# A decoder's second attention on one core: where it begins behind the expert feed, and what runs in its first stages

## The reference, cut to what matters

```
x = layernorm(x + L0_attn(x))        # retention
x = layernorm(x + L0_xattn(x, ctx))  # attention to the context, then W_out
x = layernorm(x + L0_ffn(x))         # 64 experts, top 8 of each token, and 2 shared experts
x = layernorm(x + L1_attn(x))        # linear attention with a memory (64 wide)
x = layernorm(x + L1_xattn(x, ctx))  # keys = ctx @ W_k, values = ctx @ W_v, 16 heads
x = layernorm(x + L1_ffn(x))         # 8 gated experts, top 2 of each token
```

## Time and profile before

| | us |
|---|---|
| median of 3 runs | 1998.11 |
| lowest, highest | 1990.38, 2002.12 |
| profiled execution, its own time | 2008.36 |
| profiled execution, span of the core | 2005.4 |
| TensorE matmuls busy in the span | 1712.4 (85%) |
| VectorE busy | 1165.6 (58%) |
| ScalarE busy | 622.8 (31%) |
| GpSimd busy | 894.2 (45%) |
| mean granted clock of TensorE | 0.912 of full speed |

### The profile page before, as it was taken

One profiled execution on the slowest core, in us unless ns is written; L12 is line 12 of the kernel. 1 busy time (PEld: TensorE's weight loads), 2 busy tenths in 40 slices (PEclk: granted clock), 3 DMA queues, 4 the chain that ended last, 5 costly groups with the idle time before them and its releaser, 6 DMA issues.

```text
span 2005.4 us, 45537 instructions
## 1 busy us (share of the span) xinstructions
PE 1712.4 (85%) x17739; PEld 1345.2 (67%) x17739; DVE 1165.6 (58%) x3228; ACT 622.8 (31%) x957; POOL 894.2 (45%) x1000
## 2 busy tenths in 40 slices
PE   6788888888789889998998478999977499999994
PEld 5576666666556666675776356676656499999994
DVE  3576655665441276766656466787764345655564
ACT  1232322222231276454455123454332111111110
POOL 0017556754758102888887865333322202222223
PEclk9998988998699999999999688899987699999997
DMA  9415543555349799897999822114101512333332
GB/s 322 148 47 195 185 149 110 193 183 187 131 149 252 204 298 304 257 285 259 299 306 304 288 86 62 55 64 148 44 33 54 172 49 75 90 93 94 100 93 68
DMA packets 269634, 322.61 MB, mean 161 GB/s; under 512 B 25083, under 2 KB 245487, under 8 KB 268655
## 3 DMA queue, kind: packets, MB, share of 16 engines
q1 hardware_dynamic: 234559, 226.38, 35.7%
q0 software_dynamic: 33024, 92.32, 14.2%
q10 hardware_dynamic: 1840, 1.00, 0.2%
HBM read 157.22 MB, written 162.40 MB: 159 GB/s over the span
## 4 chain that ended last, share of the span: by engine, by line
PE 69%; DVE 8%; issue 6%; DMA 5%; POOL 4%; ACT 4%; another core or an unknown queue 2%; SPq 1%; DVEq 0%; POOLq 0%; ACTq 0%
PE wide L2065 13%; PE d_yp L2077 6%; PE wide L1197 4%; PE wide L110 4%; PE wide L127 4%; PE wide L1200 4%; PE bank L1210 3%; PE bank L1217 3%; PE e_yp L1737 3%; PE wide L1726 3%; PE bank L1031 2%; PE wide L1184 2%; POOL big L1439 2%; PE e_xp L1714 2%; PE bank L1174 2%
## 5 line engine op out<-in xcount | busy, mean ns | idle before, releaser
L1439 POOL DMA_INDIRECT big<-results,slots x256 | 263.2, 1028 | 208.6 <-DMA results<-e_y 128.5
L2065 PE MATMUL wide<-d_xt,d_ws 128*128 128x128 f32 x2272 | 278.0, 276 | 0.6 <-issue 0.6
L2065 PEld LDWEIGHTS wide<-d_xt,d_ws 128*128 128x128 f32 x2272 | 271.7, 193 | 4.5 <-issue 1.0
L597 POOL DMA_INDIRECT lists<-big,slots x160 | 159.3, 995 | 117.7 <-DVE slots L959 71.3
L661 ACT ACTIVATE pt<-wide 77x2048 f32<-77x2048 f32 x64 | 119.9, 1873 | 216.0 <-PE wide L1200 125.0
L1934 POOL DMA_INDIRECT d_picked<-results,slots x64 | 64.1, 1002 | 181.1 <-DMA results<-d_y 167.8
L1965 ACT ACTIVATE d_gate<-wide 128x512 f32<-128x512 f32 x71 | 42.4, 597 | 324.2 <-PE wide L2065 319.6
L1454 DVE SCALAR_TENSOR_TENSOR big<-big,weights 128x256 f32<-128x256 f32 x256 | 109.2, 488 | 43.8 <-DMA big<-results,slots 30.0
L2077 PE MATMUL d_yp<-d_wd,d_h 128*128 x568 | 134.2, 379 | 0.0
L110 PE MATMUL wide<-shared_sx,shared_sw 128*128 128x512 f32 x256 | 127.4, 621 | 5.4 <-DMA shared_sx<-res_t 2.9
L127 PEld LDWEIGHTS wide<-shared_sw,shared_sh 128*128 128x128 f32 x512 | 98.1, 192 | 45.1 <-issue 29.3
(11 more groups left out here) (280 smaller groups left out, 3511.5 us busy)
## 6 DMA issues: line engine op xcount, KB each, us to landing
lists<-zero SPq DMA_DIRECT2D x20, 2048.0 KB, 14.8
e_x<-lists SPq DMA_DIRECT2D x80, 512.0 KB
results<-e_y SPq DMA_DIRECT2D x80, 512.0 KB
d_x<-lists SPq DMA_DIRECT2D x71, 128.0 KB
results<-d_y SPq DMA_DIRECT2D x71, 128.0 KB
e_w<-in_L_w SPq DMA_DIRECT2D x2, 4096.0 KB
shared_sw<-in_x_t SPq DMA_DIRECT2D x32, 128.0 KB
x<-in_x SPq DMA_DIRECT2D x8, 512.0 KB
```

The costliest lines, as they stand in the source:

```text
L597: pool.indirect_dma_start(out=lists, out_offset=bass.IndirectOffsetOnAxis(ap=slots[:, b, i, k:k + 1], axis=0), in_=z2[i % 3][:, b, :], in_ ...
L1439: pool.indirect_dma_start(out=picked[:, c % NG, b, :], out_offset=None, in_=results[0:-(-PAGES_OF_STEP[s] // 4) * 4 * R0, :], in_offset=ba ...
L2065: ins = mm(out[T % 2][:, a * P:(a + 1) * P], ws[:, T % NW, n, c, a * P:(a + 1) * P], xt[:, T % 2, c], start=c == 0, stop=c == KC - 1)
```

## The change

- The feed hands on `y_done` (last eviction done) in place of the landing of the last stores and of the shared experts' base; the stores' landing is waited for by VectorE at the first top. The sync queue's own waits for them at the feed's end go.
- The second attention's constants come in two lots. `consts_soon`: on the sync queue, behind x of step 0, ident, the three linear weights and the memory; on ScalarE's queue causal, gate, head_mask, mem_norm and the output weight. `consts`: context, wk, wv on the sync queue, the rest on ScalarE's. TensorE, ScalarE and VectorE begin behind the first lot; GpSimd waits for all at its first ln1, TensorE at the first key.
- The keys' products become jobs of the order, behind num (0, 1), x0t (1, 1), lv 1 and ct 0; TensorE waits for all four laid out before the first mx.
- One late sum (46) stands ahead of `begin_here` instead of three. 47 is behind tri (0, 1), 48 behind x0t (1, 1), 49 behind wo (0, 1), then three in a round for steps 0 to 4: behind x1t (i, 1), mx (i, 0) and mx (i, 3).

```diff
+def with_keys(order):
+    behind = [("num", 0, 1), ("x0t", 1, 1), ("lv", 1, 0), ("ct", 0, 0)]
+    out = []
+    for job in order:
+        out.append(job)
+        if job in behind:
+            out.append(("key", behind.index(job), 0))
+    return out
 def with_late(order):
-    behind = [("x0t", 0, 1), ("sig", 0, 0)]
-    for i in range(4):
-        behind += [("x1t", i, 1), ("q", i, 1), ("mx", i, 1), ("mx", i, 3)]
-    behind = behind[:STEPS * K0 + 1 - LATE - 3]
-    out, n = [], STEPS * K0 + 1 - len(behind)
+    behind = [("tri", 0, 1), ("x0t", 1, 1), ("wo", 0, 1)]
+    for i in range(5):
+        behind += [("x1t", i, 1), ("mx", i, 0), ("mx", i, 3)]
+    out, n = [], LATE + 1
...
-            loads = [context, (wk[:], col(d["wk"])), (wv[:], col(d["wv"]))] + loads
-            loads += [(wlin[:, :, 0], col(d["wq1"])), (wlin[:, :, 1], col(d["wk1"])), (wlin[:, :, 2], col(d["wv1"])),
-                      (mem_norm[:], d["mem_norm_rows"])]
-            others = [(gate[:], d["gate"])] + others + [(wq[:], col(d["wq"])), (iota[:], d["iota"])]
+            soon = [loads[0]] + [(wlin[:, :, n], col(d[w])) for n, w in enumerate(("wq1", "wk1", "wv1"))]
             for h in range(2):
                 rows_h = slice(h * MEM, (h + 1) * MEM)
-                others += [(wo[rows_h], d["wo1"])]
-                loads += [(memory[rows_h, 0:MEM], d["memory"]), (memory[rows_h, MEM:], d["mem_norm"])]
+                soon += [(memory[rows_h, 0:MEM], d["memory"]), (memory[rows_h, MEM:], d["mem_norm"])]
+            soon_too = [(causal[:], d["causal"]), (gate[:], d["gate"]), loads[1], (mem_norm[:], d["mem_norm_rows"])]
+            soon_too += [(wo[h * MEM:(h + 1) * MEM], d["wo1"]) for h in range(2)]
+            loads = [context, (wk[:], col(d["wk"])), (wv[:], col(d["wv"]))]
+            others = [(wq[:], col(d["wq"]))] + others[1:] + [(iota[:], d["iota"])]
...
             load_t(0)
+            if not first:
+                load(0)
             for dst_ap, src_ap in soon:
                 sp.dma_start(dst_ap, src_ap).then_inc(consts_soon, 16)
...
             if not first:
-                for n in range(LATE, LATE + 3):
-                    late_on_pool(pool, n)
+                late_on_pool(pool, LATE)
             begin_here(pool)
...
                 if stage == "ln1" and not first:
+                    if i == 0:
+                        pool.wait_ge(consts, CONSTS)
...
+            for dst_ap, src_ap in soon_too:
+                act.dma_start(dst_ap, src_ap).then_inc(consts_soon, 16)
...
-                act.wait_ge(consts, CONSTS)
+                act.wait_ge(consts_soon, SOON)
...
             if not first:
-                for n in range(LATE, LATE + 3):
-                    late_on_vector(dve, n)
+                late_on_vector(dve, LATE)
             begin_here(dve)
...
+                if stage == "key":
+                    ps = filled(dve, job)
+                    lay_out_keys(i, ps[:, 0:KC * CTX].rearrange("p (c k) -> p c k", c=KC), ps[0:CTX, DM:2 * DM])
...
                 if stage == "top":
+                    if i == 0:
+                        for of_before, count in stores:
+                            dve.wait_ge(of_before, count)
...
             begin_here(pe)
-            if first:
-                pe.wait_ge(consts_soon, 16 * len(soon))
-            else:
-                pe.wait_ge(consts, CONSTS)
-                for b in range(NB):
-                    out = take_bank(("key", b, 0))
...
+            pe.wait_ge(consts_soon, SOON)
...
-            else:
-                pe.wait_ge(ready, READY)
             for job in order:
...
+                if not first and job == ("key", 0, 0):
+                    pe.wait_ge(consts, CONSTS)
+                if not first and job == ("num", 0, 0):
+                    pe.wait_ge(ready, BEGUN)
+                if job == ("mx", 0, 0):
                     pe.wait_ge(ready, READY)
+                    for b in range(0 if first else NB):
+                        emptied(pe, ("key", b, 0))
...
             store_quad(QUADS - 1)
-            for n in range(NY):
-                sp.wait_ge(sent[n], 16 * len(range(n, QUADS, NY)))
-            sp.wait_ge(base_sent, 16 * STEPS)
...
-        return over, kept, late_on_pool, late_on_vector
+        return [(y_done, QUADS)], over, kept, late_on_pool, late_on_vector
```

More of the change, by code:

```diff
@@ L200, in with_late @@
             n += 1
+    assert n == STEPS * K0 + 1
     return out
@@ L229, in attention_phase @@
                     spare=None, route=None, block=None,
-                    over=(), kept=(), late_on_pool=None, late_on_vector=None, units=None):
+                    over=(), stores=(), kept=(), late_on_pool=None, late_on_vector=None, units=None):
     first = layer == 0
-    order = with_units(steady(SEQUENCE0)) if first else with_late(steady(SEQUENCE1))
-    prep_jobs = [] if first else [(("key", b, 0), "narrow") for b in range(NB)]
-    plan = Banks(prep_jobs + bank_jobs(order), {"wide": ["w"], "narrow": [0, 1, 2, 3]}, shared.uses)
+    order = with_units(steady(SEQUENCE0)) if first else with_late(with_keys(steady(SEQUENCE1)))
+    plan = Banks(bank_jobs(order), {"wide": ["w"], "narrow": [0, 1, 2, 3]}, shared.uses)
     score_scale = 1.0 if first else float(XD) ** -0.5
@@ L368, in attention_phase @@
         consts = sem("consts")
-        consts_soon = sem("consts_soon") if first else None
+        consts_soon = sem("consts_soon")
         ready = sem("ready")
@@ L472, in _ @@
             load_t(0)
+            if not first:
+                load(0)
             for dst_ap, src_ap in soon:
                 sp.dma_start(dst_ap, src_ap).then_inc(consts_soon, 16)
-            load(0)
+            if first:
+                load(0)
             for dst_ap, src_ap in loads:
@@ L723, in _ @@
             if first:
[L724 removed]
+                dve.wait_ge(consts_soon, SOON)
                 make(nc.vector.reciprocal(scale_qk[:, 2:4], scale_qk[:, 0:2]))
@@ L731, in lay_out @@
             def lay_out():
-                dve.wait_ge(consts, CONSTS)
+                if first:
+                    dve.wait_ge(consts, CONSTS)
+                else:
+                    dve.wait_ge(consts_soon, SOON)
                 make(nc.vector.tensor_reduce(mask2[:], head_mask[:].rearrange("p (m h) -> p h m", h=2), AX.X, ALU.add))
@@ L990, in _ @@
             begin_here(pe)
-            if first:
-                pe.wait_ge(consts_soon, 16 * len(soon))
-            else:
-                pe.wait_ge(consts, CONSTS)
-                for b in range(NB):
-                    out = take_bank(("key", b, 0))
-                    for g in range(KC):
-                        for c in range(KC):
-                            mm(out[:, g * CTX:(g + 1) * CTX], wk[:, c, g * P:(g + 1) * P], ctx_t[:, b, c],
-                               start=c == 0, stop=c == KC - 1)
-                    for c in range(KC):
-                        ins = mm(out[0:CTX, DM:2 * DM], ctx_t[:, b, c], wv[:, c], start=c == 0, stop=c == KC - 1)
-                    fills(ins, ("key", b, 0))
+            pe.wait_ge(consts_soon, SOON)
             if first:
                 pe.wait_ge(state_done, 1)
-            else:
-                pe.wait_ge(ready, READY)
             for job in order:
@@ L1027, in _ @@
                     out = take_bank(job)
+                if stage == "key":
+                    for g in range(KC):
+                        for c in range(KC):
+                            mm(out[:, g * CTX:(g + 1) * CTX], wk[:, c, g * P:(g + 1) * P], ctx_t[:, i, c],
+                               start=c == 0, stop=c == KC - 1)
+                    for c in range(KC):
+                        ins = mm(out[0:CTX, DM:2 * DM], ctx_t[:, i, c], wv[:, c], start=c == 0, stop=c == KC - 1)
+                    fills(ins, job)
                 if stage == "qk":
```

39 lines of the change are left out of this document (20 added, 19 removed).

## The result

| | before | after |
|---|---|---|
| median, 20 runs each, us | 2002.05 | 2009.37 |
| lowest, highest | 1990.38, 2010.85 | 2001.99, 2020.48 |
| profiled execution, its own time | 2008.36 | 2007.76 |
| span of the core | 2005.4 | 2005.7 |

The ratio is 1.0039, 95% interval [1.0025, 1.0054]: the kernel after is **slower by 0.4%**, some 7 us, where 9 us less was forecast, and outside the range.

The account below looks back on a forecast made before the run. No engine fills the span, so the prediction read the hand-over hole alone, where TensorE waits for loads. 11 us gained at the start less 2 lost in the rounds gave 9 us, a median of 1989 us, range 1980 to 1998.

Parts of the forecast that it names:

- Start of TensorE, 1127.5 (1126.5 to 1130): At the hand-over: TensorE begins at 1127.5 instead of 1137.43, taking 5.0 us from the last piece's issue to use.
- First stages at half clock, +2.7: Transposes and linear products before the numerator run on an unwarmed array, 2.7 us longer (bounds 0 and 4).
- Keys, 6.7 us: Four keys' products between numerator and output product lengthen TensorE's path by 6.7 us (bounds 5 and 12).
- ln1 of step 0 at 1161.1: First layernorm of step 0 taken up by GpSimd at 1161.1 instead of 1172.06, 11 us gained.
- Late sums three a round, 2 lost (bounds 6 lost, 1 gained): Dense rounds of steps 0 to 4: two more sums and a norm, spread thinner, lose 2 us.
- rival C: Start paid late: late first lot, keys at half clock, or GpSimd holding ln1; gain about 2 us, 1996; chance 0.23.
- Nothing at the end: Behind the rounds: the gated phase moves as a block; no loss at the kernel's end was priced.
- D: Slower: step 7's late store holds up the second weights and x of step 7; 10 us slower, 2008; chance 0.05.
- E: Second lot lands after 1145, so TensorE idles at key 0 instead; gain 3 to 5 us, 1994; chance 0.05.
- five rounds of 47 us or more: Sign that would prove the forecast wrong; rounds of steps 0 to 4 were expected at some 45 us each.

Follow-up runs that it names:

- e1: Kernel after with its late sums from the 50th on placed as in the kernel before, four a round; ratio 0.9971 to before.
- e2: Kernel before with only the late sums' places of the kernel after, three a round over five rounds; ratio 1.0095 to before.
- e8: Kernel after with eight more small memsets on idle GpSimd; ratio 1.0002 to before.
- e14: Kernel after with four late sums a round in steps 1 to 3, two of them where VectorE idles; ratio 0.9956 to before.
- e10: As e14, but the last late job (norm and store of step 7) moved into step 4's round; ratio 1.0021 to before.
- e16: The same kernel as e14, run on a chip where before takes 2015.9 us; ratio 1.0000 to before.
- e17: The same kernel as e10, run on a chip where before takes 2015.9 us; ratio 1.0035 to before.

## Why the prediction was wrong, point by point

*Start of TensorE, 1127.5 (1126.5 to 1130): inside the bounds.* 1128.60. The whole of this profile lies 0.8 us earlier than before's at this point (ScalarE's last eviction at 1114.41, not 1115.22), so the forecast on its time base is 1126.7. The last piece was issued at 1121.90, as forecast on that base (1121.7), but issue to use took 6.7 us instead of 5.0. By the Trainium skill's rule of interleaving (DMA: Bandwidth & Descriptors, "Issuing engines are not separate DMA queues") it would have been 1130; the trace lies between the two.

*First stages at half clock, +2.7: right.* The granted clock was 0.50 from 1128 to 1134 and 1.00 from 1136. The transposes took 1.94 for 1.09 and the linear products 4.87 for 2.81; from the start to the end of the numerator it was 12.9 us (1128.60 to 1141.53), 13.0 forecast. The Trainium skill's sentence that the default state is throttled (TensorE: Matmul & The Clock Gate, "What's actually happening") spoke against this change here, and the trace agrees.

*Keys, 6.7 us: too high by 2.6.* Numerator to output product took 13.3 us where before took 9.15, so 4.2. The keys' own 7.3 us of TensorE were priced right. What the sum left out is that the slow stretch of before is not there: the 16 linear products behind the second key took 1.95 us, 3.68 before, as the granted clock was 1.00 all along, where before it was 0.50 from 1160 to 1164. That the keys' work keeps it up is likely but not tried.

*ln1 of step 0 at 1161.1: right, in part by luck.* 1159.56, and GpSimd's last gather ahead of it ended at 1156.06, where I put it. Measured from the feed's last product 11.7 us were gained; forecast 11. The number is so close because two misses cancel: TensorE began 1.9 us late on the profile's own base, and the keys' stretch was 2.6 us shorter than forecast.

***Late sums three a round, 2 lost (bounds 6 lost, 1 gained): this is the step that failed.*** Five rounds cost 13.9 us more. By the medians the places of the late sums as a whole cost 10 us (after against e1, from different groups of runs, ratios 0.0068 apart) or 16 (e2 against before, 0.0095), each less 0.0016 for the tail. I wrote that "nearly the same work is spread thinner" and priced it by the us, from what I called two rounds of 47.3 us; the two maxima are the ends of one. It broke in three places:
- Each us of late work was priced by what it cost where four sums stood in a round, 0.74 us of path (5.9 for 8). In after, step 3's round has 6.4 us of it (three sums of 1.67 and the norm's 1.37) and is 7.5 longer than before's: 1.2 us of path for each. Step 4's has 3.0 us of it and is 5.0 longer. In step 3 one sum and the norm stand ahead of the second peak, in step 4 one sum, and TensorE's third maximum waits 3.0 and 3.2 us for it, 0.43 in before.
- The clock was left out of the rounds, though rival C had it at the start. Step 2's round holds three sums too and took 42.9 at 1.00; step 3's took 49.0 at 0.90. A mean of 0.90 is 9.8 us at 1.2 GHz, in which half the work is done: up to 4.9 us, my estimate, of the 6.1 between them; the norm's 1.4 could be the rest. The hole of 1.51 us stands right ahead of the fall; behind the one of 2.99 the clock stayed at 1.00 for another 9 us. So that the holes cost the clock is argued, not shown.
- I let the thinner rounds pay for the two new ones. Rounds 3 and 4, free in before, came in at 49.0 and 48.1 instead of 41.5 and 43.1 (13.1 us by the means of the pairs), and rounds 0 to 2, with three sums for four, gave nothing back (0.8 us longer in all).

*Nothing at the end: wrong.* The tail grew by 3.3 us, all in GpSimd's closing DRAIN (6.56 us before, 9.83 after). No step spoke of it.

*Rivals.* D did not come: the second weights went out at 1385.73 (1387.19 before). C's half clock at the keys and E's hole at key 0 did not come either. The other side came by a mechanism that I had as a bound and not as a rival: "five rounds of 47 us or more" stood among what would prove me wrong, and rounds 0, 1, 3 and 4 were that in the first profile. But before's own rounds 1 and 2 took 48.0 and 47.3, so only rounds 3 and 4 answer that sign.

*What stays open.* Why GpSimd's last DRAIN takes 9.8 us in all eleven profiles in which late work reaches step 4's round and 6.6 in all nine in which it ends in step 3's. And how much of the rounds' loss is the clock's: the split above is read from traces, not tried. It seems to differ by chip: e8, with after's places on a chip where before takes 1870, has waits of 2.8 and 3.4 us ahead of the same two maxima, and its rounds 3 and 4 take 42.5 and 43.5 us against 36.3 for a free one, at 0.96 and 0.97. By the same estimate the clock is at most 1.7 of the 6.2 us there.

## What to carry to other kernels

Work put into another phase's in-order stream costs what it delays there, so price it at its place: what bank or operand does the next instruction free, and who waits for it. A hole on TensorE may be paid a second time by the clock behind it (above, up to 4.9 us in one round, my estimate), so look at each round's granted clock beside its length. One part of a change may need another (the early start gave nothing until the sums were out of its head), while a third (the spread) can be taken back: try each alone before either is called good or bad. The best mixture here won 0.4% on two chips and nothing on a third, and e1 0.3% on a fourth, so no version is shown to beat the kernel before everywhere.

## What the runs showed of the hardware

The kernel before takes 1870 us on the chips numbered 0 and 1 and 2002 on number 10; under number 15 it took 2002 us in one group and 2016 in another. In a round without late sums (36.3 us against 41.5) the score products show it. Of the two timelines of TensorE below, the first is e14 where before takes 1869 us, the second the kernel after:

```profile
1312.91 0.40 PE L1220 MATMUL wide<-shared_sw,keys 32*77 32x128 f32 x8
1313.13 0.40 PE L1223 MATMUL wide<-peak_t,sel 32*77 32x128 f32 x8
1313.35 0.40 PE L1220 MATMUL wide<-shared_sw,keys 32*77 32x128 f32 x8
1313.57 0.40 PE L1223 MATMUL wide<-peak_t,sel 32*77 32x128 f32 x8
1313.89 1.08 PE L1233 MATMUL bank<-pt,vals 77*32 77x128 f32 x32
1314.90 1.99 PE L1197 MATMUL bank<-x1t,wq 128*128 128x512 f32 x4
```

```profile
1438.74 0.47 PE L1220 MATMUL wide<-shared_sw,keys 32*77 32x128 f32 x4 [0.27 <-issue]
1439.50 0.45 PE L1220 MATMUL wide<-shared_sw,keys 32*77 32x128 f32 x4 [0.29 <-issue]
1440.23 0.37 PE L1223 MATMUL wide<-peak_t,sel 32*77 32x128 f32 x3 [0.27 <-issue]
1441.67 0.49 PE L1223 MATMUL wide<-peak_t,sel 32*77 32x128 f32 x5 [1.07 <-issue]
1442.09 1.38 PE L1233 MATMUL bank<-pt,vals 77*32 77x128 f32 x32
1443.40 3.33 PE L1197 MATMUL bank<-x1t,wq 128*128 128x512 f32 x4
```

On the slower chip TensorE stands still between small products with nothing to wait for that the profile shows, 0.27 to 1.07 us at a time, and then the clock falls (granted 1.00 up to 1442, 0.58 during the query's products): these four take 3.33 us, not 1.99. Counting such stands of over 0.25 us among these products, the rounds of steps 1 to 5 have 3 to 7 each in every profile where before takes 2002 us or more, with late sums or without, save step 1's round in e10, e16 and e17, which has none; the profiles where it takes 1870 have none in these rounds. What holds TensorE there is not in the trace.
